# One fused attention-and-gate kernel: rows parted at 512 instead of 416, last part in chunks of 128, 128 and 32 rows, inverse roots spread through memory

## The chip, the cores and the metric

The kernel runs on one core of a Trainium2 chip. The metric is the device time in microseconds of the whole launch, the median of three runs. A span is the time from the first to the last instruction in one profiled execution; the launch takes a little more than its span.

## The reference

For 8 batches of N = 100 rows (R = 800 rows in all), width D = 1024, each with a memory of 722 rows of width 512:

```
memory_proj    = memory @ W_mem.T
attn           = softmax(hidden @ memory_proj.T / sqrt(D))
memory_context = attn @ memory_proj
gate           = sigmoid(concat(hidden, memory_context) @ W_gate.T + b_gate)
fused          = hidden + gate * memory_context
out            = fused * rsqrt(mean(fused**2, axis=-1) + 1e-6) * norm_w
```

All is float32. The last line needs, for each of the 800 rows, a mean over all 1024 columns before any value of that row can be written.

## The kernel before

Each float32 operand is split in a high part (rounded for TensorE's faster float32 form) and a low part, and each product is three matmuls: high by high, high by low, low by high (`three`, L314). The first 214 us of the span are the projections, the attention of the eight batches and the context times the memory weights. They are not changed.

Then comes the gate stage. Data lies transposed: partitions are columns of the model (KD = 8 tiles `t` of P = 128), the free dimension is the rows. The list `STEPS` sets its order: 17 steps `(t, r0, r1)`, each one tile of output columns for a range of rows, each 24 matmuls (8 tiles of the contraction, three products each) into one of two PSUM banks. The rows are in two parts, the first 416 rows and the last 384. The steps of the first part end at step END0 = 8; only (0, late) comes among them. Then follow the steps of the last part, the final one cut in 256 and 128 rows.

For each step, in pipeline with TensorE: ScalarE (ACT) takes the sigmoid out of PSUM (L694), seeds the bank of the step after next with the part of the gate that was made earlier (L700), takes squares (L713) and multiplies by norm_w in place (`weigh`, L704). VectorE (DVE) multiplies the gate by the context (L887), adds the input (`fuse`, L892) and adds the squares up (`sum_squares`, L875). `gate` and `square` have two buffers each, so a sigmoid waits for the fuse of two steps before, and a step's matmuls wait for their seed.

When all eight tiles of the first part are summed, TensorE makes its means (`mean_first`, L495, in the middle of step 10, after its contraction tile 4); DVE adds epsilon (L920), GpSimd (POOL) takes the power -1/2 (L969). These inverse roots lie by rows on partitions and are wanted along the free dimension on all partitions: DVE makes four diagonal matrices (L898), TensorE multiplies them by ones into bank RIB (`inverse`, L503, in the middle of step 11), and DVE multiplies each of the eight tiles by that bank (`output`, L904), two after each step from step 12 on. The sync engine (SP) stores two tiles at a time (L298), its queue in order: the last weight loads, then these four stores, then the row stores.

The last part ends by rows: TensorE makes the means of three chunks of 128 rows (L527, L532, L533) and transposes their tiles into PSUM (`turn`, L515); ACT scales the left half of the rows (L734) and DVE the right half (L949) by the inverse root into `row_out`, and SP stores each chunk of 512 KB (L302). The last wait of the kernel is for all stores.

Of the kernel before, what the change touches and what calls it, by code (L numbers as in the profile page):

```python
# [22 lines left out]
FIRST, CHUNK = 416, 128  # L23
ROWS2, LATE = (R - FIRST) // CHUNK, R - CHUNK
FC = FIRST // 4

TURN = ((0, 1), (2, 3), (5, 4))
# [9 lines left out]
    + [(t, FIRST, R) for t in range(1, KD - 1)] + [(KD - 1, FIRST, LATE), (KD - 1, LATE, R)]  # L37
# [8 lines left out]
def build(nc, xT, ctxT, ctxN, w_mem, w_gate_x, w_mem_t, w_gate_mc, b_gate, norm_w, outT, out_rows):  # L46
# [4 lines left out]
    with top:  # L51
# [47 lines left out]
        ones = sb(top, "ones", [P, P])  # L99
        minus_half = sb(top, "minus_half", [P, 4])  # L100
        rms = sb(top, "rms", [FC, 4])
        rms_late = sb(top, "rms_late", [CHUNK, ROWS2])
        rms_diag = sb(top, "rms_diag", [FC, 4, FC])
# [10 lines left out]
        row_out = x_again.rearrange("p k r -> p (k r)")[0:CHUNK, 0:ROWS2 * D]  # L114
# [69 lines left out]
        diag_done = sem("diag_done")  # L184
        inv_made = sem("inv_made")
        mean_w_set = sem("mean_w_set")
        late_mean_made = sem("late_mean_made")
        late_squared = sem("late_squared")
# [14 lines left out]
        def _(sp):  # L203
# [90 lines left out]
            for t in range(1, KD):  # L294
                load_w(J_G2 + t, w_gate_mc[t], t % 2)
            for k in range(0, KD, 2):
                sp.wait_ge(out_done, k + 2)
                sp.dma_start(out_v[:, k:k + 2, :], acc[:, k:k + 2, 0:FIRST]).then_inc(stored, 16)  # L298
            for i in range(ROWS2):
                sp.wait_ge(row_left, i + 1)  # L300
                sp.wait_ge(row_right, i + 1)
                sp.dma_start(out_rows[i * CHUNK:(i + 1) * CHUNK, :],  # L302
                             row_out[:, i * D:(i + 1) * D]).then_inc(stored, 16)
            sp.wait_ge(stored, 16 * (KD // 2 + ROWS2))
# [3 lines left out]
        def _(pe):  # L308
# [198 lines left out]
            def late_sums(i):  # L507
                at = FIRST + i * CHUNK
                return square_sum[:, at:at + CHUNK]

            def turn(i, t0, t1):

                at = FIRST + i * CHUNK
                for t in range(t0, t1):
                    done = nc.tensor.transpose(bank(TURN[i][t // 4], P, CHUNK, t % 4 * P), acc[:, t, at:at + CHUNK],  # L515
                                               ident[:, :])
# [487 lines left out]
```

## Time and profile before

| what | value |
|---|---|
| median of 3 runs | 298.63 us (298.62 to 299.34) |
| the profiled execution | 297.93 us |
| its span | 296.0 us, outside it 1.93 us |
| TensorE busy | 290.2 us, 98% |
| VectorE busy | 169.1 us, 57% |
| ScalarE busy | 159.9 us, 54% |
| gate stage, first matmul to last | 214.22 to 287.04 us |
| first and last row store issued | 290.38 and 292.16 us |

Times of instructions are microseconds from the start of the span. In the profile's rows PE is TensorE's matmul side, PEld its weight loads, SPq the sync engine's queue. Busy times of pipelined matmuls overlap, so the distance from one matmul's start to the next one's start, not the busy time, is what a matmul costs.

### The profile page before, as it was taken

What the parts mean: (1) busy time and instruction counts of PE and PEld (TensorE: products, weight loads), DVE (VectorE), ACT (ScalarE), POOL (GpSimd) and SP (SyncE); (2) the same over time, 40 slices, a digit from 0 to 9 for tenths busy, and PEclk for the clock granted to TensorE, in tenths of its full rate; (3) what the DMA queues carried; (4) which work ended last, traced back from release to release, by engine and by line L of the source; (5) the groups of instructions that cost most, each with busy time, mean ns of one, the idle gap of its engine ahead of it and who ended that gap; (6) DMA issues with size and microseconds to landing.
All of it is one profiled execution on the core that took longest, in us unless ns stands there. A gap on an engine that the chain in (4) does not pass through costs nothing.

```text
span 296.0 us, 4113 instructions
## 1 busy us (share of the span) xinstructions
PE 290.2 (98%) x1666; PEld 279.4 (94%) x1666; DVE 169.1 (57%) x234; ACT 159.9 (54%) x227; POOL 4.0 (1%) x10
## 2 busy tenths in 40 slices
PE   8999999999999999999999999999999999999993
PEld 8999999898999989899998989999999999999992
DVE  3658554558576575856657544422467662443663
ACT  5548435554574835448473526454367674543563
POOL 2000000000000000000000000000000000010001
PEclk9999999999999999999999999999999999999998
DMA  6999180884929569293966121086223400000235
GB/s 213 405 404 284 56 319 16 242 280 122 329 80 291 227 159 358 83 321 124 269 249 160 56 75 42 31 338 248 73 75 137 142 3 0 0 2 16 99 117 213
DMA packets 20930, 49.29 MB, mean 167 GB/s; under 512 B 2688, under 2 KB 4480, under 8 KB 20912
## 3 DMA queue, kind: packets, MB, share of 16 engines
q1 hardware_dynamic: 20912, 49.04, 49.4%
q8 instruction: 13, 0.21, 0.3%
q14 instruction: 5, 0.04, 0.0%
HBM read 45.49 MB, written 3.28 MB: 165 GB/s over the span
## 4 chain that ended last, share of the span: by engine, by line
PE 98%; DVE 0%; issue 0%; DVEq 0%
PE ps L314 70%; PE ps L408 11%; PE ps L431 9%; PE ps L422 1%; PE ps L435 1%; PE ps L328 1%; PE ps L442 1%; PE ps L515 1%; PE ps L503 0%; PE ps L339 0%; DVE x_again L949 0%; PE ps L345 0%; PE ps L349 0%; PE ps L342 0%; PE ps L354 0%; PE ps L351 0%
## 5 line engine op out<-in xcount | busy, mean ns | idle before, releaser
L314 PE MATMUL ps<-act_hi,w_hi 128*128 128x400 f32 (+4 forms) x272 | 79.8, 343 | 0.0
L314 PE MATMUL ps<-act_hi,w_lo 128*128 128x400 f32 (+4 forms) x272 | 79.0, 340 | 0.0
L314 PE MATMUL ps<-act_lo,w_hi 128*128 128x400 f32 (+4 forms) x272 | 78.9, 340 | 0.0
L314 PEld LDWEIGHTS ps<-act_hi,w_hi 128*128 128x128 f32 x272 | 49.9, 188 | 1.0
L314 PEld LDWEIGHTS ps<-act_lo,w_hi 128*128 128x128 f32 x272 | 50.6, 188 | 0.1
L314 PEld LDWEIGHTS ps<-act_hi,w_lo 128*128 128x128 f32 x272 | 50.6, 188 | 0.1
L741 DVE TENSOR_TENSOR w_lo<-w_stage,w_hi 128x1024 fp32r<-128x1024 f32 (+2 forms) x23 | 26.0, 1132 | 23.8 <-ACT w_hi L550 23.0
L741 DVE TENSOR_TENSOR cn_lo<-cn_stage,cn_hi 128x1536 fp32r<-128x1536 f32 (+1 forms) x16 | 23.8, 1486 | 7.2 <-ACT cn_hi L569 5.6
L741 DVE TENSOR_TENSOR ct_lo<-ct_stage,ct_hi 128x1444 fp32r<-128x1444 f32 x16 | 25.8, 1653 | 0.5 <-ACT ct_hi L561 0.5
L550 ACT ACTIVATE w_hi<-w_stage 128x1024 fp32r<-128x1024 f32 x20 | 21.0, 1054 | 6.0 <-PE ps L314 3.9
L637 ACT ACTIVATE pc<-ps,row_inv 100x512 f32<-100x512 f32 x8 | 5.5, 688 | 31.6 <-PE ps L435 31.6
L694 ACT ACTIVATE gate<-ps,bias_t 128x384 f32<-128x384 f32 (+3 forms) x15 | 8.6, 570 | 24.8 <-PE ps L314 24.7
L561 ACT ACTIVATE ct_hi<-ct_stage 128x1444 fp32r<-128x1444 f32 x16 | 21.7, 1405 | 0.0
L623 ACT ACTIVATE probs<-ps,neg_top 100x722 f32<-100x722 f32 x8 | 6.9, 865 | 27.2 <-DVE neg_top L820 27.2
L887 DVE TENSOR_TENSOR gate<-gate,mc 128x416 f32<-128x416 f32 (+3 forms) x17 | 9.3, 550 | 21.2 <-ACT gate L694 21.2
L408 PE MATMUL ps<-ct_hi,q_hi 128*100 128x362 f32 x64 | 21.4, 335 | 0.0
L408 PE MATMUL ps<-ct_hi,q_lo 128*100 128x362 f32 x64 | 21.0, 328 | 0.0
L408 PE MATMUL ps<-ct_lo,q_hi 128*100 128x362 f32 x64 | 21.0, 328 | 0.0
L741 DVE TENSOR_TENSOR act_lo<-mc,act_hi 128x800 fp32r<-128x800 f32 x8 | 7.9, 993 | 20.5 <-ACT mc L665 20.5
L314 PE MATMUL ps<-q_hi,w_hi 128*128 128x400 f32 x64 | 17.5, 344 | 0.0
L314 PE MATMUL ps<-q_lo,w_hi 128*128 128x400 f32 x64 | 17.5, 344 | 0.0
L314 PE MATMUL ps<-q_hi,w_lo 128*128 128x400 f32 x64 | 17.4, 344 | 0.0
(113 smaller groups left out, 459.9 us busy)
## 6 DMA issues: line engine op xcount, KB each, us to landing
ct_stage<-ctxT SPq DMA_DIRECT2D x16, 722.0 KB, 8.4
cn_stage<-ctxN SPq DMA_DIRECT2D x8, 768.0 KB, 5.8
cn_stage<-ctxN SPq DMA_DIRECT2D x8, 512.0 KB, 4.2
w_stage<-w_gate_x SPq DMA_DIRECT2D x8, 512.0 KB, 6.1
w_stage<-w_gate_mc SPq DMA_DIRECT2D x8, 512.0 KB, 3.5
x_again<-xT SPq DMA_DIRECT2D x1, 3200.0 KB, 11.5
cn_stage<-ctxN SPq DMA_DIRECT2D x8, 320.0 KB
acc<-xT SPq DMA_DIRECT2D x6, 400.0 KB, 7.4
```

The costliest lines, as they stand in the source:

```text
L314: done = nc.tensor.matmul(o, wgt, stream[h][part], start=first and wgt is wh and part == 0, stop=last and wgt is wl, skip_group_check=onto)
L328: nc.tensor.matmul(bank(7, P), idle_work[:, :], idle_work[:, :], start=True, stop=True)
L408: done = nc.tensor.matmul(bank(h, MH + 1, N), lhs[:, k, b * N:(b + 1) * N], rhs[:, k, at:at + MH + 1], start=k == 0 and part == 0, stop=k ...
L422: done = nc.tensor.transpose(o, probs[:, t * P:t * P + rows], ident[0:N, 0:N])
L431: nc.tensor.matmul(bank(PCB, C, N), lhs[:, t, :], rhs[:, t, :], start=t == 0 and part == 0, stop=False)
L550: nc.scalar.activation(w_hi[home][:, :], w_stage[:, slot, :], ACT.Copy).then_inc(w_hi_done, 1)
L561: nc.scalar.activation(ct_hi[:, 2 * s:2 * s + 2, :], ct_stage[:, 2 * s:2 * s + 2, :], ACT.Copy).then_inc(ct_hi_done, 1)
L623: nc.scalar.activation(probs[:, :].rearrange("p (h m) -> p h m", h=2), scores, ACT.Exp, bias=neg_top[:, :], scale=float(D) ** -0.5, accum_ ...
L637: nc.scalar.activation(pc[:, :], bank(PCB, C, N), ACT.Copy, scale=row_inv[:, :]).then_inc(pc_scaled, 1)
L694: nc.scalar.activation(part, part if n < 2 else gate_bank(n), ACT.Sigmoid, bias=bias_t[:, t:t + 1]).then_inc(gate_done, 1)
L741: return nc.vector.tensor_tensor(out, whole, hi.bitcast(F32), ALU.subtract)
L887: nc.vector.tensor_tensor(part, part, mc[:, t, r0:r1], ALU.mult).then_inc(gated, 1)
```

## The change

The first part has 512 rows and the last 288. The final step is no longer cut for TensorE, so there are 16 steps. The last part ends in chunks of 128, 128 and 32 rows (`CHUNKS`). Everything after the last matmul is done chunk by chunk: three sigmoids, three pairs of product and sum, squares on ACT instead of DVE, and means that add the sums of the tiles before to the squares of the last tile. The 32 rows of the small chunk are weighed into a buffer `small`, so that two transposes give 32 rows by 1024 columns on all 128 partitions as (row, quarter of the columns); their store is one contiguous piece of 128 KB. The means of the first part are made after contraction tile 1 of step 10, not tile 4. The inverse roots of the first part are stored to scratch memory `rms_rows` (128 by 4) and loaded back to all partitions (`rms_all`); the diagonals, the ones and the matmuls `inverse` are gone, and `output` reads `rms_all` with a step of four elements. The core of the diff:

```diff
...
-FIRST, CHUNK = 416, 128
-ROWS2, LATE = (R - FIRST) // CHUNK, R - CHUNK
...
+FIRST, SMALL = 512, 32
+CHUNKS = ((FIRST, FIRST + P), (FIRST + P, FIRST + 2 * P), (R - SMALL, R))
+PAIRS = P // SMALL
+NC = len(CHUNKS)
...
-TURN = ((0, 1), (2, 3), (5, 4))
+TURN, MEANS = ((0, 1), (2, 3), (5, 6)), (6, 7, 4)
...
-    + [(t, FIRST, R) for t in range(1, KD - 1)] + [(KD - 1, FIRST, LATE), (KD - 1, LATE, R)]
+    + [(t, FIRST, R) for t in range(1, KD)]
 LAST = len(STEPS) - 1
...
-        G2B, RIB = 4, 3
-
-        def late_mean(i, n=1):
-            return bank(6, n, CHUNK, 8 + i) if i < ROWS2 - 1 else bank(7, n, CHUNK, BANK - 1)
+        G2B = 4
+
+        def late_mean(i):
+            return bank(MEANS[i], 1, P, 8)
+
+        def small_part(t):
+            return small[:, t % 2, t // 2:P:PAIRS]
...
+            sp.wait_ge(rooted, 1)
+            sp.dma_start(rms_rows, rms[:, :]).then_inc(rms_stored, 16)
+            sp.wait_ge(rms_stored, 16)
+            sp.dma_start(rms_all[:, :], rms_rows.rearrange("p i -> (p i)").partition_broadcast(P)).then_inc(rms_in, 16)
             for k in range(0, KD, 2):
                 sp.wait_ge(out_done, k + 2)
                 sp.dma_start(out_v[:, k:k + 2, :], acc[:, k:k + 2, 0:FIRST]).then_inc(stored, 16)
...
+                if i < NC - 1:
+                    sp.dma_start(out_rows[i * P:(i + 1) * P, :],
+                                 row_out[:, i * D:(i + 1) * D]).then_inc(stored, 16)
+                else:
+                    sp.dma_start(out_rows[i * P:i * P + SMALL, :].rearrange("r (u c) -> (r u) c", u=PAIRS),
+                                 row_out[:, i * D:i * D + D // PAIRS]).then_inc(stored, 16)
...
-            def inverse():
-
-                pe.wait_ge(diag_done, 4)
-                for i in range(4):
-                    done = nc.tensor.matmul(bank(RIB, FC, P, i * FC), ones[0:FC, :], rms_diag[:, i, :],
-                                            start=True, stop=True)
-                done.then_inc(inv_made, 1)
...
+            def mean_of_sums(i):
+
+                a, b = CHUNKS[i]
+                pe.wait_ge(summed, LAST if i < NC - 1 else LAST + 1)
+                nc.tensor.matmul(late_mean(i), square_sum[:, a:b] if i < NC - 1 else small_sum[:, 0, :], mean_w[:, :],
+                                 start=True, stop=False)
+
+            def mean_of_last(i):
+
+                a, b = CHUNKS[i]
+                pe.wait_ge(squared, LAST + 1 + i)
+                nc.tensor.matmul(late_mean(i), square[:, LAST % 2, a - FIRST:b - FIRST] if i < NC - 1
+                                 else small_sum[:, 1, :], mean_w[:, :], start=False, stop=True)                    .then_inc(late_mean_made, 1)
...
+            def turn_small():
+
+                for j in range(2):
+                    done = nc.tensor.transpose(bank(TURN[NC - 1][j], P), small[:, j, :], ident[:, :])
                 return done
 
             for n in range(END0 + 2):
                 gate_mc(n)
-            gate_mc(END0 + 2, 4, mean_first)
-            gate_mc(END0 + 3, 4, inverse)
-            for n in range(END0 + 4, LAST + 1):
+            gate_mc(END0 + 2, 1, mean_first)
+            for n in range(END0 + 3, LAST + 1):
                 gate_mc(n)
-            pe.wait_ge(summed, LAST)
-            for i in range(ROWS2 - 1):
-                done = nc.tensor.matmul(late_mean(i), late_sums(i), mean_w[:, :], start=True, stop=True)
-            done.then_inc(late_mean_made, 1)
             pe.wait_ge(weighted, LAST)
-            turn(0, 0, KD).then_inc(turned, 1)
-            pe.wait_ge(late_squared, 1)
-            nc.tensor.matmul(late_mean(ROWS2 - 1), late_sums(ROWS2 - 1), mean_w[:, :], start=True, stop=False)
-            nc.tensor.matmul(late_mean(ROWS2 - 1), square[:, LAST % 2, 0:CHUNK], mean_w[:, :],
-                             start=False, stop=True).then_inc(late_mean_made, 1)
-            pe.wait_ge(out_done, KD)
-            turn(1, 0, KD).then_inc(turned, 1)
+            turn(0, 0, KD - 1)
+            mean_of_sums(0)
+            mean_of_sums(1)
+            turn(1, 0, 1)
+            mean_of_last(0)
+            turn(1, 1, 4)
+            mean_of_last(1)
             pe.wait_ge(weighted, LAST + 1)
-            turn(2, 0, KD).then_inc(turned, 1)
+            turn(0, KD - 1, KD).then_inc(turned, 1)
+            turn(1, 4, KD - 1)
+            mean_of_sums(2)
+            pe.wait_ge(weighted, LAST + 2)
+            turn(1, KD - 1, KD).then_inc(turned, 1)
+            mean_of_last(2)
+            pe.wait_ge(weighted, LAST + NC)
+            pe.wait_ge(mean_copied, 2)
+            turn_small().then_inc(turned, 1)
...
             def weigh(n):
                 t, r0, r1 = STEPS[n]
+                if r1 == R:
+                    nc.scalar.activation(small_part(t), acc[:, t, R - SMALL:R], ACT.Copy, scale=norm_t[:, t:t + 1])
+                    r1 = R - SMALL
                 nc.scalar.activation(acc[:, t, r0:r1], acc[:, t, r0:r1], ACT.Copy,
                                      scale=norm_t[:, t:t + 1]).then_inc(weighted, 1)
...
-            act.wait_ge(late_squared, 1)
-            weigh(LAST)
-            for i in range(ROWS2):
-                act.wait_ge(late_rooted, 1 + (i == ROWS2 - 1))
+            finish(LAST - 1)
+            act.wait_ge(gate_made, LAST + 1)
+            act.wait_ge(fused, LAST - 1)
+            for a, b in CHUNKS:
+                at = slice(a - FIRST, b - FIRST)
+                nc.scalar.activation(gate[:, LAST % 2, at], gate_bank(LAST)[:, at], ACT.Sigmoid,
+                                     bias=bias_t[:, KD - 1:KD]).then_inc(gate_done, 1)
+            act.wait_ge(summed, LAST - 1)
+            for i, (a, b) in enumerate(CHUNKS):
+                part = acc[:, KD - 1, a:b]
+                act.wait_ge(fused, LAST + 1 + i)
+                if i < NC - 1:
+                    nc.scalar.activation(square[:, LAST % 2, a - FIRST:b - FIRST], part,
+                                         ACT.Square).then_inc(squared, 1)
+                else:
+                    nc.scalar.activation(small_sum[:, 1, :].rearrange("p (r u) -> p r u", u=PAIRS),
+                                         part.unsqueeze(2).to_broadcast([P, SMALL, PAIRS]),
+                                         ACT.Square).then_inc(squared, 1)
+                act.wait_ge(squared, LAST + 1 + i)
+                nc.scalar.activation(part if i < NC - 1 else small_part(KD - 1), part, ACT.Copy,
+                                     scale=norm_t[:, KD - 1:KD]).then_inc(weighted, 1)
+            for i in range(NC):
+                act.wait_ge(late_rooted, i + 1)
                 act.wait_ge(turned, i + 1)
-                nc.scalar.activation(row_out[:, i * D:i * D + BANK], bank(TURN[i][0], BANK, CHUNK), ACT.Copy,
+                turned_left = bank(TURN[i][0], BANK if i < NC - 1 else P)
+                nc.scalar.activation(row_out[:, i * D:i * D + turned_left.shape[1]], turned_left, ACT.Copy,
                                      scale=rms_late[:, i:i + 1]).then_inc(row_left, 1)
...
-            def diagonals():
-                dve.wait_ge(rooted, 1)
-                for i in range(4):
-                    nc.vector.tensor_scalar(rms_diag[:, i, :], ident[0:FC, 0:FC], rms[:, i:i + 1], None,
-                                            ALU.mult).then_inc(diag_done, 1)
-
             def output(k):
 
-                rows = acc[:, k, 0:FIRST]
-                nc.vector.tensor_tensor(rows, rows, bank(RIB, FIRST), ALU.mult).then_inc(out_done, 1)
+                rows = acc[:, k, 0:FIRST].rearrange("p (i f) -> p i f", i=4)
+                nc.vector.tensor_tensor(rows, rows, rms_all.rearrange("p (f i) -> p i f", i=4),
+                                        ALU.mult).then_inc(out_done, 1)
...
             dve.wait_ge(mean_made, 1)
             nc.vector.tensor_scalar(rms[:, :], bank(6, 4, FC), EPS, None, ALU.add).then_inc(mean_copied, 1)
-            diagonals()
...
                 if n == END0 + 3:
                     dve.wait_ge(weighted, END0 + 1)
-                    dve.wait_ge(inv_made, 1)
+                    dve.wait_ge(rms_in, 16)
                 while done < min(KD, 2 * (n - END0 - 2)):
                     output(done)
...
+            for i, (a, b) in enumerate(CHUNKS):
+                part = gate[:, LAST % 2, a - FIRST:b - FIRST]
+                dve.wait_ge(gate_done, LAST + 1 + i)
+                nc.vector.tensor_tensor(part, part, mc[:, KD - 1, a:b], ALU.mult).then_inc(gated, 1)
+                dve.wait_ge(gated, LAST + 1 + i)
+                nc.vector.tensor_tensor(acc[:, KD - 1, a:b], part, x_again[:, KD - 1, a:b],
+                                        ALU.add).then_inc(fused, 1)
+            dve.wait_ge(summed, LAST)
+            nc.vector.tensor_copy(small_sum[:, 0, :].rearrange("p (r u) -> p r u", u=PAIRS),
+                                  square_sum[:, R - SMALL:R].unsqueeze(2).to_broadcast([P, SMALL, PAIRS]))                .then_inc(summed, 1)
+
+            def late_mean_plus_eps(i):
+                dve.wait_ge(late_mean_made, i + 1)
+                nc.vector.tensor_scalar(rms_late[:, i:i + 1], late_mean(i), EPS, None, ALU.add).then_inc(mean_copied, 1)
...
-            late_mean_plus_eps(1, ROWS2 - 1, 1)
-            for i in range(ROWS2):
-                right_half(i)
+            late_mean_plus_eps(0)
+            late_mean_plus_eps(1)
+            right_half(0)
+            late_mean_plus_eps(2)
+            right_half(1)
+            right_half(2)
...
```

## Rows read from the trace of the kernel before

**Rows 1.** The profile's first part (busy time, share, instructions), and the granted clock in 40 slices.

```profile
PE 290.2 (98%) x1666; PEld 279.4 (94%) x1666; DVE 169.1 (57%) x234; ACT 159.9 (54%) x227; POOL 4.0 (1%) x10
...
PEclk9999999999999999999999999999999999999998
```

**Rows 2.** Chain that ended last, in order of time: start, us, what.

```profile
261.75 0.65 PE ps L495 x8
...
266.73 0.87 PE ps L503 x8
...
289.42 1.82 PE ps L515 x16
...
291.33 0.75 DVE x_again L949
```

**Rows 3.** Timeline of ACT: start, us, instruction, idle time before and its releaser.

```profile
250.47 0.61 ACT L694 ACTIVATE gate<-ps,bias_t 128x416 f32<-128x416 f32 x1 [2.22 <-PE ps L314]
255.00 0.61 ACT L694 ACTIVATE gate<-ps,bias_t 128x416 f32<-128x416 f32 x1 [2.25 <-PE ps L314]
...
257.20 0.54 ACT L713 ACTIVATE square<-acc 128x416 f32<-128x416 f32 x1
...
273.52 0.58 ACT L694 ACTIVATE gate<-ps,bias_t 128x384 f32<-128x384 f32 x1 [2.01 <-PE ps L314]
...
277.73 0.58 ACT L694 ACTIVATE gate<-ps,bias_t 128x384 f32<-128x384 f32 x1 [2.01 <-PE ps L314]
```

**Rows 4.** Timeline of PE: first matmul of four steps, and the last of all.

```profile
254.74 0.34 PE L314 MATMUL ps<-act_hi,w_hi 128*128 128x384 f32 x1
...
281.69 0.28 PE L314 MATMUL ps<-act_hi,w_hi 128*128 128x256 f32 x1
...
284.53 0.22 PE L314 MATMUL ps<-act_hi,w_hi 128*128 128x128 f32 x1
...
287.04 0.28 PE L314 MATMUL ps<-act_hi,w_lo 128*128 128x128 f32 x1
```

**Rows 5.** Timeline of PE, 512 columns wide: the first and the 16th of one row of matmuls.

```profile
139.01 0.39 PE L431 MATMUL ps<-cn_hi,pt_hi 128*100 128x512 f32 x1
...
142.49 0.40 PE L435 MATMUL ps<-cn_hi,pt_hi 124*100 124x512 f32 x1
```

**Rows 6.** Timeline of DVE, second half of the gate stage.

```profile
257.76 0.59 DVE L875 TENSOR_TENSOR square_sum<-square_sum,square 128x416 f32<-128x416 f32 x1 [0.40 <-ACT square L713]
...
282.56 0.56 DVE L887 TENSOR_TENSOR gate<-gate,mc 128x384 f32<-128x384 f32 x1 [1.60 <-ACT gate L694]
...
284.10 1.08 DVE L904 TENSOR_TENSOR acc<-acc,ps 128x416 f32<-128x416 f32 x2
```

**Rows 7.** Groups of DVE by shape: count, busy us, mean ns, idle before.

```profile
L741 DVE TENSOR_TENSOR w_lo<-w_stage,w_hi 128x1024 fp32r<-128x1024 f32 x20 | 24.5, 1225 | 23.0 <-ACT w_hi L550 23.0
...
L904 DVE TENSOR_TENSOR acc<-acc,ps 128x416 f32<-128x416 f32 x8 | 4.3, 581 | 0.0
...
L741 DVE TENSOR_TENSOR w_lo<-w_stage,w_hi 128x512 fp32r<-128x512 f32 x1 | 0.7, 693 | 0.2 <-ACT w_hi L588 0.2
```

**Rows 8.** Timeline of POOL.

```profile
262.75 1.03 POOL L969 TENSOR_TENSOR rms<-rms,minus_half 104x4 f32<-104x4 f32 x1 [260.29 <-DVE rms L920]
...
289.69 0.55 POOL L973 TENSOR_TENSOR rms_late<-rms_late,minus_half 128x1 f32<-128x1 f32 x1 [0.69 <-DVE rms_late L936]
```

**Rows 9.** Timeline after the last step: the last tile's product, sum and weighing.

```profile
288.14 0.29 DVE L892 TENSOR_TENSOR acc<-gate,x_again 128x128 f32<-128x128 f32 x1
...
288.79 0.40 ACT L704 ACTIVATE acc<-acc,norm_t 128x128 f32<-128x128 f32 x1 [1.01 <-DVE square L944]
```

**Rows 10.** Timeline of SP's queue, the row stores.

```profile
290.38 2.11 SPq L302 DMA_DIRECT2D out_rows<-x_again  x3
```

**Rows 11.** DMA of 289 to 296 us in 40 slices, and the issues by line.

```profile
DMA  0000000000004999999999999999999999600000
GB/s 0 0 0 0 0 0 0 0 0 0 0 0 164 398 421 421 398 374 398 398 398 492 398 398 374 374 421 375 421 421 421 374 468 445 234 0 0 0 0 0
```

**Rows 12.** DMA issues of the whole span, in groups: KB each, us from issue to landing.

```profile
outT<-acc SPq DMA_DIRECT2D x4, 416.0 KB, 2.5
```

More of the change, by code:

```diff
@@ L98, in build @@
         mean_w = sb(top, "mean_w", [P, 1])
-        ones = sb(top, "ones", [P, P])
         minus_half = sb(top, "minus_half", [P, 4])
         rms = sb(top, "rms", [FC, 4])
-        rms_late = sb(top, "rms_late", [CHUNK, ROWS2])
-        rms_diag = sb(top, "rms_diag", [FC, 4, FC])
+        rms_late = sb(top, "rms_late", [P, NC])
+        small = sb(top, "small", [P, 2, P])
+        small_sum = sb(top, "small_sum", [P, 2, P])
+        rms_all = sb(top, "rms_all", [P, FIRST])
+        rms_rows = nc.dram_tensor("rms_rows", (FC, 4), F32, kind="Internal").ap()
         w_hi.append(sb(top, "w_hi2", [P, WB], F32R))
@@ L717, in _ @@
             act.wait_ge(gx_saved, 2 * B)
-            for n in range(LAST + 1):
+            for n in range(LAST):
                 if n in SPLIT_AT:
                     split_gate_w(SPLIT_AT[n])
-                early = n == END0 + 1 or n >= LAST - 1
+                early = n == END0 + 1
                 if early:
@@ L728, in _ @@
                     finish(n - 1)
-            act.wait_ge(late_squared, 1)
-            weigh(LAST)
-            for i in range(ROWS2):
-                act.wait_ge(late_rooted, 1 + (i == ROWS2 - 1))
+            finish(LAST - 1)
[19 more added lines that the diff above has]
+                                     scale=norm_t[:, KD - 1:KD]).then_inc(weighted, 1)
+            for i in range(NC):
+                act.wait_ge(late_rooted, i + 1)
                 act.wait_ge(turned, i + 1)
-                nc.scalar.activation(row_out[:, i * D:i * D + BANK], bank(TURN[i][0], BANK, CHUNK), ACT.Copy,
+                turned_left = bank(TURN[i][0], BANK if i < NC - 1 else P)
+                nc.scalar.activation(row_out[:, i * D:i * D + turned_left.shape[1]], turned_left, ACT.Copy,
                                      scale=rms_late[:, i:i + 1]).then_inc(row_left, 1)
@@ L847, in _ @@
             nc.vector.memset(mean_w[:, :], 1.0 / D).then_inc(mean_w_set, 1)
-            nc.vector.memset(ones[:, :], 1.0).then_inc(mean_w_set, 1)
             nc.vector.memset(minus_half[:, :], -0.5).then_inc(mean_w_set, 1)
@@ L933, in _ @@
             sum_squares(LAST - 1)
-            def late_mean_plus_eps(late, at, n):
-                dve.wait_ge(late_mean_made, late + 1)
-                nc.vector.tensor_scalar(rms_late[:, at:at + n], late_mean(at, n), EPS, None,
-                                        ALU.add).then_inc(mean_copied, 1)
-            gate_times(LAST)
-            late_mean_plus_eps(0, 0, ROWS2 - 1)
-            fuse(LAST)
-            part = acc[:, KD - 1, LATE:R]
-            dve.wait_ge(fused, LAST + 1)
-            nc.vector.tensor_tensor(square[:, LAST % 2, 0:CHUNK], part, part, ALU.mult).then_inc(late_squared, 1)
+            for i, (a, b) in enumerate(CHUNKS):
[5 more added lines that the diff above has]
+                                        ALU.add).then_inc(fused, 1)
@@ L964, in _ @@
             nc.gpsimd.memset(cn_stage[96:P, MT:MT + 2, :], 0.0).then_inc(spare_zeroed, 1)
-            pool.wait_ge(mean_w_set, 4)
+            pool.wait_ge(mean_w_set, 3)
             pool.wait_ge(mean_copied, 1)
             nc.gpsimd.tensor_tensor(rms[:, :], rms[:, :], minus_half[0:FC, :], ALU.pow).then_inc(rooted, 1)
-            for late, at, n in ((0, 0, ROWS2 - 1), (1, ROWS2 - 1, 1)):
-                pool.wait_ge(mean_copied, late + 2)
-                part = rms_late[:, at:at + n]
-                nc.gpsimd.tensor_tensor(part, part, minus_half[0:CHUNK, 0:n], ALU.pow).then_inc(late_rooted, 1)
+            for i in range(NC):
+                pool.wait_ge(mean_copied, i + 2)
+                part = rms_late[:, i:i + 1]
+                nc.gpsimd.tensor_tensor(part, part, minus_half[:, 0:1], ALU.pow).then_inc(late_rooted, 1)
 def kernel(x, ctx_1024, L0_xattn_W_mem, L0_xattn_W_gate, L0_xattn_b_gate, L0_xattn_norm_w):
```

28 lines of the change are left out of this document (11 added, 17 removed).

## The prediction

> **What bounds the kernel now.** I read the page first: TensorE is busy 98% of the span, at a granted clock of 9 tenths or more in all slices but the last [rows 1]. The reader should see that DVE (57%) and ACT have room on average, so that only two things can move the time: what TensorE is given to do, and what comes after its last matmul. The chain of waits says the same: it runs along TensorE to the transposes at 289.42, one DVE operation follows, and the rest is the store [rows 2]. The timeline of the gate stage shows no gap at the change of steps. So I price matmuls by the distance between starts.
>
> Per step of 24 matmuls: 416 columns take 4.53 us (255.00 less 250.47), 384 take 4.21 (277.73 less 273.52) [rows 3], 256 take 2.84 (284.53 less 281.69), and 128 take 2.62 (287.04 less 284.53 is 23 distances, 0.109 each) [rows 4]. Per matmul that is 189, 175, 118 and 109 ns. Halving 256 columns to 128 saves almost nothing: there the weight load sets the distance. All of the stage: 8 x 4.53 + 7 x 4.21 + 2.84 + 2.62 = 71.2 us, beside 1.5 us of other matmuls. I call T the end of the matmuls, 287.15 (287.04 + 0.11). From T to the end of the span are 8.85 us, and 1.93 us lie outside the span of this execution (297.93 us). The median is 0.7 above it; I carry my differences over to the median.
>
> **The new widths.** 512 columns: a row of matmuls in the attention has 15 distances in 3.48 us, 232 ns each [rows 5], so 5.57 us a step. Its weights have 100 columns and not 128, but at 232 ns a load is hidden either way. 288 columns: no row has them; between 256 (118) and 384 (175) the line gives 133 ns, 3.18 us a step. Bounds: 2.9 (the rate of 128 columns and the slope, were it bent) and 3.3. New sum: 8 x 5.57 + 8 x 3.18 = 70.0 us. **Gain 1.2 us**, of which nearly all is the step of 128 columns that is gone. With the bounds: from 0.2 to 2.
>
> **The matmuls of the inverse** are gone: 0.87 us in the chain [rows 2], all on TensorE. **Gain 0.87.** The memset of `ones` and the diagonals on DVE lay beside matmuls: nothing.
>
> **The means sooner.** They cost 0.65 [rows 2] for weights of 104 columns; with 128 about 0.75. Can they start? Before, the step after the first part starts at 254.74 [rows 4], its sigmoid 0.26 later, the last square at 257.20 [rows 3], the last sum at 257.76, ending 258.35 [rows 6], which is 3.6 after 254.74. The chain on ACT holds now a sigmoid, one square and one weighing of 512 columns and a seed of 288: +0.1 three times and -0.1; the last square and the last sum add 0.1 each. So the sum is ready at 4.0. TensorE comes there after one narrow step and six matmuls, 3.18 + 0.80 = 3.98, and loads weights 0.13 ahead. I take a stall of 0.15; bounds 0 and 0.6 (one more ACT operation ahead, such as the additional weighing of 32 columns that each late step now has). **Cost 0.25 with the wider weights.** Behind the wait stand all later matmuls, so it is paid in full.
>
> **The way through memory.** From the start of step 9: means made at 4.9, epsilon, then the power on POOL, 1.03 us [rows 8], 6.2; SP is past its weight loads and issues the store at 6.3. Behind the wait for it stand on SP only the output stores, which need the load anyway. No row has a store of 2 KB; the nearest is 416 KB in 2.5 us [rows 12]. I take 2.5 each for store and load (256 KB); bounds 1.5 and 5. `rms_all` is there at about 11.5. DVE wants it after the sum in step 11's pipeline: three narrow steps, the means, a sigmoid and three DVE operations, 12.7. So 1.2 us of cover, and DVE has more later (next paragraph). The wait costs nothing up to about 8.6 us for both, while gate products queue behind it on DVE.
>
> **DVE's load per narrow step.** Before, product to end of the two outputs is 282.56 to 285.18, 2.62 us in 4.21 [rows 6]. Now: three operations of 288 (about 0.46, distance 0.38 to 0.49) and two outputs of 512 columns. Contiguous, 512 columns take 0.69 [rows 7], distance 0.64: 2.5 us in a step of 3.18. Four such groups, steps 11 to 14; the last leaves DVE free at T+0.5 and the first chunk's sigmoid is done at T+0.64. Room in all: 3 x 0.68 + 0.15 = 2.2 us. But `rms_all` is read with a step of four elements, 16 bytes, and no row shows such a read. Bounds for one output: 0.69, and 1.22 for the row of 1024 columns [rows 7], as if each element cost two; beyond that a rival. I take 0.69, since all DVE rows here, from PSUM too (416 columns 0.58), go at one column in 1.04 ns [rows 7]. Cost 0.
>
> The Trainium skill (SBUF — State Buffer, section on the DMA port swizzle, its note on cachelines) says that lines are 16 bytes and that accesses which cross to a new line each time pay a penalty, full bandwidth needing two hits a line. No row here has it. By that rule every element of this read is a new line and the output goes up by an amount that the page doesn't give; it is rival A.
>
> **The tail.** Before, the first row store issues at T+3.2, the third at T+5.0 [rows 10], and data flows without a gap from 291.2 to 295.1 (T+7.95), 1.57 MB at about 400 GB/s [rows 11]: the stores' flow is the tail, once it has begun. After: sigmoid T+0.27 to 0.64; product and sum to 1.28 (0.29 each, distance 0.33 [rows 9]); ACT's square to 1.63; the mean's last matmul to 2.1; DVE is in the copy for the small chunk until 2.35, then epsilon to 2.5; POOL 0.55 [rows 8] to 3.15; the right half 0.75 [rows 2] to 3.9. First store T+4.0, later by 0.8. ACT's left half waits until its three squares and weighings (0.3 to 0.4 apart [rows 9]) are done at 3.25. Second chunk 4.85 (epsilon of the third goes ahead of it), third 5.25. TensorE's transposes (0.11 each [rows 2]) fit between. But only 1.18 MB are left to flow: 2.95 us from T+4.75 (0.8 after the issue) ends at T+7.7. **Gain 0.25**; bounds: -1.2 (each of the six waits between engines 0.25 later) and +0.6.
>
> **The sum.** -1.2 - 0.87 + 0.25 - 0.25 = -2.1 us: the profiled execution 295.9, the median 296.5 us.
>
> **Rivals.**
> A: the stepped read costs two columns' time each. 8 x 0.53 = 4.3 us more on DVE, less the room of 2.2: DVE comes to the last tile 2.1 late, the tail slides by it, 298.6 us, no change. For it: the read touches a line per element. Against: DVE's rate is the same from all its sources here, and that a second operand's fetch limits it is nowhere seen.
> B, the other side: the same read costs more still. With e us more per output, it is slower than before by 0.9 once 8e is over 2.2 + 2.1 + 0.9, so e over 0.65 and an output over 1.34 us. At 2.5 columns' time, e = 0.8: 6.4 - 2.2 = 4.2, 300.7 us. DVE would then be the bound of steps 11 to 14. Against: no DVE row goes slower than 1.4 ns per column.
> C: the tail's chain. ACT, DVE and TensorE hand over three chunks in a fixed order, and TensorE's in-order waits hold transposes back. At the bound, +1.45 against my sum, 298.0 us. For it: the chain before had four handovers for its last chunk, this one has them for each. Against: each is worked out above and stores overlap.
>
> **How the numbers follow.** Forecast 0.60, A 0.22, B 0.07, C 0.11. Less than 0.3% (0.9 us, 297.7 to 299.5) can't be told from no change. Faster: most of the forecast (0.58), 0.04 of C, 0.02 of A: 0.64. Same: 0.24. Slower: B, 0.04 of A, 0.01 of C: 0.12. Range 295.6 to 299.0; the forecast's own is 295.6 to 297.4.
>
> **What would show it.** A step of the first part 5.5 to 5.6 us between sigmoids, of the last 3.1 to 3.3; if 3.4, the widths gain nothing. L495's successor with a wait below 0.3 us before its weight load. Outputs of 128x512: 0.69 us right, 1.2 is A, over 1.34 is B. `rms_all` landing about 5 us after the power; if over 8.6, DVE stalls. First row store 4.0 us after the last gate matmul ends, data flowing to 7.7; if the last landing is later than before against T, C. The forecast is wrong if the median is above 297.7.

## The result and the profile after

The changed kernel takes 297.10 us (median of 6 runs, 296.70 to 297.55), the kernel before 298.62 (298.33 to 299.34). The ratio is 0.9947, 95% interval 0.9937 to 0.9958, so a gain of 1.3 to 1.9 us. Forecast were 296.5 and a gain of 2.1.

The page, and the sigmoids of two 512-column and two 288-column steps, to be compared with [rows 1, 3]:

```profile
PE 289.1 (98%) x1632; PEld 269.6 (91%) x1632; DVE 171.1 (58%) x231; ACT 161.0 (54%) x237; POOL 4.3 (1%) x11
...
PEclk9999999999999999999999999999999999999997
```

```profile
240.78 0.69 ACT L718 ACTIVATE gate<-ps,bias_t 128x512 f32<-128x512 f32 x1 [2.18 <-PE ps L328]
...
246.35 0.69 ACT L718 ACTIVATE gate<-ps,bias_t 128x512 f32<-128x512 f32 x1 [1.99 <-PE ps L328]
...
273.71 0.50 ACT L718 ACTIVATE gate<-ps,bias_t 128x288 f32<-128x288 f32 x1 [1.13 <-PE ps L328]
...
276.91 0.50 ACT L718 ACTIVATE gate<-ps,bias_t 128x288 f32<-128x288 f32 x1 [1.13 <-PE ps L328]
```

A step of 512 columns takes 5.57 us between sigmoids, one of 288 takes 3.20. Then the ends of the stage, on PE (start, us):

```profile
266.68 0.29 PE L328 MATMUL ps<-act_hi,w_lo 128*128 128x288 f32 x1
266.86 1.05 PE L509 MATMUL ps<-mean_w,square_sum 128*128 128x1 f32 x8
267.77 0.38 PE L328 MATMUL ps<-act_hi,w_hi 128*128 128x288 f32 x1
...
286.09 0.30 PE L328 MATMUL ps<-act_hi,w_lo 128*128 128x288 f32 x1
```

The gate matmuls end at T = 286.09 + 0.13 = 286.22. They began at 215.01, where before they began at 214.22; nothing ahead of that point is changed, and other profiles of the same kernel begin the stage at 214.60 and 214.42. So the stage is read by its length: 71.21 us against 72.93, **1.72 us less**. The store of the roots, their load and DVE's steps (SP, then DVE):

```profile
269.49 0.33 SPq L303 DMA_DIRECT2D rms_rows<-rms  x1
271.43 0.33 SPq L305 DMA_DIRECT2D rms_all<-rms_rows  x1
...
290.79 1.06 SPq L313 DMA_DIRECT2D out_rows<-x_again  x2
```

```profile
275.11 0.45 DVE L921 TENSOR_TENSOR square_sum<-square_sum,square 128x288 f32<-128x288 f32 x1
275.48 2.10 DVE L944 TENSOR_TENSOR acc<-acc,rms_all 128x512 f32<-128x512 f32 x2
277.46 0.49 DVE L933 TENSOR_TENSOR gate<-gate,mc 128x288 f32<-128x288 f32 x1
...
285.16 2.12 DVE L944 TENSOR_TENSOR acc<-acc,rms_all 128x512 f32<-128x512 f32 x2
287.19 0.46 DVE L921 TENSOR_TENSOR square_sum<-square_sum,square 128x288 f32<-128x288 f32 x1
287.56 0.29 DVE L977 TENSOR_TENSOR gate<-gate,mc 128x128 f32<-128x128 f32 x1
```

The reader should see that two outputs of 512 columns take 2.1 us, not 1.3, that DVE goes from the outputs at once into the next product from 277.46 on, without the idle time that ended at 282.56 in [rows 6], and that the product of the last tile's first chunk starts at 287.56, 1.34 us after T. The chain that ended last ran along TensorE up to one last DVE operation before [rows 2]; now it leaves TensorE four steps of the last part before T, and from 275.11 on it is DVE's up to the inverse roots of the last rows (start, us, what):

```profile
267.91 5.71 PE ps L328 x42
...
286.17 1.11 DVE acc L944
287.28 0.37 DVE square_sum L921
...
291.39 0.37 ACT x_again L781
```

The first row store is issued at T+4.57 (290.79) and the span ends at T+9.4, before T+3.2 and T+8.85. **The tail (all that comes after T) costs 0.5 us more**, where 0.25 less was forecast.

### The profile page after: what moved, and what is told of

It reads as the page before. It is cut to its first block, busy times and chain, and to the rows that moved or that the text cites. A ratio compares the mean times of both kernels' runs of the same rounds, so it can differ in the third digit from the quotient of the medians.

```text
span 295.6 us, 4053 instructions
## 1 busy us (share of the span) xinstructions
PE 289.1 (98%) x1632; PEld 269.6 (91%) x1632; DVE 171.1 (58%) x231; ACT 161.0 (54%) x237; POOL 4.3 (1%) x11
## 4 chain that ended last, share of the span: by engine, by line
PE 92%; DVE 4%; issue 1%; POOL 0%; ACT 0%; POOLq 0%; DVEq 0%; ACTq 0%
PE ps L328 65%; PE ps L422 11%; PE ps L445 9%; DVE acc L944 2%; PE ps L436 1%; PE ps L342 1%; PE ps L449 1%; PE ps L456 1%; DVE square_sum L921 1%; DVE gate L933 1%; PE ps L353 0%; POOL rms_late L1021 0%; PE ps L509 0%; PE ps L356 0%; DVE acc L979 0%
## 5 line engine op out<-in xcount | busy, mean ns | idle before, releaser
L328 PE MATMUL ps<-act_hi,w_hi 128*128 128x400 f32 (+2 forms) x264 | 78.0, 347 | 0.0
L328 PE MATMUL ps<-act_hi,w_lo 128*128 128x400 f32 (+2 forms) x264 | 77.2, 344 | 0.0
L328 PE MATMUL ps<-act_lo,w_hi 128*128 128x400 f32 (+2 forms) x264 | 77.2, 344 | 0.0
L328 PEld LDWEIGHTS ps<-act_hi,w_hi 128*128 128x128 f32 x264 | 48.4, 188 | 2.7
L328 PEld LDWEIGHTS ps<-act_hi,w_lo 128*128 128x128 f32 x264 | 49.0, 188 | 1.8
L328 PEld LDWEIGHTS ps<-act_lo,w_hi 128*128 128x128 f32 x264 | 49.0, 188 | 1.8
L933 DVE TENSOR_TENSOR gate<-gate,mc 128x512 f32<-128x512 f32 (+1 forms) x15 | 8.7, 583 | 19.5 <-ACT gate L718 19.5
L718 ACT ACTIVATE gate<-ps,bias_t 128x288 f32<-128x288 f32 (+1 forms) x13 | 7.6, 585 | 21.7 <-PE ps L328 21.7
```

Source lines behind the costliest of these rows:

```text
L328: done = nc.tensor.matmul(o, wgt, stream[h][part], start=first and wgt is wh and part == 0, stop=last and wgt is wl, skip_group_check=onto)
L718: nc.scalar.activation(part, part if n < 2 else gate_bank(n), ACT.Sigmoid, bias=bias_t[:, t:t + 1]).then_inc(gate_done, 1)
L933: nc.vector.tensor_tensor(part, part, mc[:, t, r0:r1], ALU.mult).then_inc(gated, 1)
```

## The experiments

Times below are medians; "of before" is the ratio to the runs of the kernel before on the same chip, with its 95% interval. T is always the start of the last gate matmul plus one distance. A line "..." in a diff marks what is left out of it.

**The changed kernel again.** No edit.

> The changed kernel as it is, run again beside the others. Both theories: 297.1 us. In its first profile the gate stage began 0.8 us later than before (215.02 against 214.22) although nothing ahead of it is changed; if that is chance, the stage begins near 214.2 here and the span is about 294.8; if it is part of the change, near 215.0 again.

297.37 us, 0.9957 of before (0.9942 to 0.9971). Its stage starts at 214.60 and is 71.21 us long; the first product stands at T+1.33, the first store at T+4.56, the end at T+9.4. The later start in the first profile doesn't repeat; the length of the stage, the first product and the first store repeat to 0.02 us.

**Contiguous reads, by the order of TensorE's weights.**

```diff
-                    ... square_sum[:, i * FC:(i + 1) * FC], mean_w[:, :],
+                    ... square_sum[:, i:FIRST:4], mean_w[:, :],
...
-                rows = acc[:, k, 0:FIRST].rearrange("p (i f) -> p i f", i=4)
-                ... rms_all.rearrange("p (f i) -> p i f", i=4), ALU.mult)
+                rows = acc[:, k, 0:FIRST]
+                ... rms_all[:, :], ALU.mult)
```

> The changed kernel with one thing else: the means take every fourth row as weights, so that the scratch memory holds the roots in the order of the rows and DVE's eight outputs read rms_all contiguously. Theory (DVE's stepped reads of 1.08 us leave it 0.7 us late at the last tile, and the tail slides by that): outputs 0.69 us, the last tile's first product 0.65 us after the last gate matmul instead of 1.34, 0.7 us faster than the changed kernel, 296.4. Rival (the stores' flow is the tail, so a late start of it is made up): outputs 0.69 but 297.1. Rival (weights read in steps cost TensorE what DVE gains): the eight matmuls of the first means over 1.3 us instead of 0.9, 297.0.

298.05 us, 0.9992 of before (0.9971 to 1.0014): no gain on the kernel before, where the changed kernel beside it had 0.9957. DVE did what the theory said:

```profile
287.90 1.29 DVE L944 TENSOR_TENSOR acc<-acc,rms_all 128x512 f32<-128x512 f32 x2
...
289.65 0.29 DVE L976 TENSOR_TENSOR gate<-gate,mc 128x128 f32<-128x128 f32 x1
```

T is 289.05, so the first product is at T+0.60, the first store (292.89) at T+3.84, the end at T+8.7: a tail 0.7 shorter. But TensorE lost more. Timeline of PE around the means, and PE in stretches (us, busy, granted clock, DMA):

```profile
267.19 2.03 PE L509 MATMUL ps<-mean_w,square_sum 128*128 128x1 f32 x8
269.08 0.38 PE L328 MATMUL ps<-act_hi,w_hi 128*128 128x288 f32 x1
...
269.49 0.44 PE L328 MATMUL ps<-act_hi,w_lo 128*128 128x288 f32 x1
269.73 0.44 PE L328 MATMUL ps<-act_hi,w_hi 128*128 128x288 f32 x1
```

```profile
263.18:266.35 3.17, 3.17 (x25) 1.00 0.00 0
269.29:272.50 3.21, 3.21 (x15) 0.51 0.02 1
```

The eight passes of weights read with a step of four take 1.9 us instead of 0.9, and right after them TensorE runs for 3.2 us at a granted clock of 0.51, its lower level of 1.2 GHz: 15 matmuls of 288 columns where the earlier stretch of the same length has 25, their starts 0.24 us apart and not 0.133. The stage is 73.71 us long, 2.50 more than the changed kernel's: 1.0 of it lies in the passes, the other 1.5 in the matmuls at the lower clock. The twelve runs fall in two groups, five of 299.4 to 299.7 and seven of 297.0 to 298.05. The profile is of the first; that the clock fell at the same place in the other four isn't shown (only their mean clocks are on record, 0.987 in three and 0.992 in one). The seven have a median of 297.7, which is the changed kernel's 297.4 with 1.0 more on TensorE and 0.7 less in the tail. So the third view of the expectation held, and something on top of it that none had.

**The old way of spreading the roots, in the new kernel.** Diagonals on DVE, ones by diagonals on TensorE in step 11 after contraction tile 4, outputs read from PSUM:

```diff
-            for n in range(END0 + 3, LAST + 1):
+            gate_mc(END0 + 3, 4, inverse)
+            for n in range(END0 + 4, LAST + 1):
...
-                ... rms_all.rearrange("p (f i) -> p i f", i=4), ALU.mult)
+                ... bank(RIB, FIRST), ALU.mult)
...
```

> The changed kernel with the old way of spreading the inverse roots: diagonals on DVE, ones by diagonals on TensorE in the middle of step 11, outputs from PSUM. Theory: TensorE has about 1.0 us more (four matmuls of 128 by 128 instead of 104), the outputs of 512 from PSUM take 0.68 us, so the tail is 0.7 earlier: 297.4, slower than the changed kernel by 0.3 us or no different. Rival (the way through memory is worth its whole 0.9 and the stepped read costs nothing): 298.0.

297.85 us, 0.9972 of before (0.9959 to 0.9985), 0.5 slower than the changed kernel beside it. Its stage is 0.9 longer (215.49 to 287.60), its outputs 0.60 apart, its first product at T+0.60 (288.20) and its first store at T+3.84 (291.44). The median alone doesn't choose between the two views, 297.4 and 298.0; the profile does: the product is in time, as the theory said. But TensorE's 0.9 and the tail's 0.7 don't cancel as far as it said. The end stands at T+8.95 and not at T+8.7 as with the contiguous reads above: of the 0.7 at the first store only 0.4 reach the end, so 0.5 are lost. The last store is issued at the same T+4.99 in both and lands 0.3 later here; why, is open.

**The way through memory alone, in the kernel before.**

```diff
-            gate_mc(END0 + 3, 4, inverse)
-            for n in range(END0 + 4, LAST + 1):
+            for n in range(END0 + 3, LAST + 1):
...
+            sp.dma_start(rms_rows, rms[:, :]) ...
+            sp.dma_start(rms_all[:, :], rms_rows.rearrange("p i -> (p i)").partition_broadcast(P)) ...
...
+                ... rms_all.rearrange("p (f i) -> p i f", i=4), ALU.mult)
```

> The kernel before with one part of the change alone: 416 rows, old tail, but the inverse roots through scratch memory with the stepped read. Theory: the inverse's 0.87 us leave TensorE and the outputs of 416, about 0.91 us each (1.80 ns a column), stay hidden, since two of them and the rest are 3.3 us in a step of 4.21: 297.7, 0.9 faster than before. Rival (a slower output slides the tail whenever it stands ahead of the last tile): 298.3 or more.

298.17 us, 0.9984 of before (0.9967 to 1.0001), so a gain of 0 to 1 us that isn't clear of none. In the profile the stage is 72.03 us, 0.90 less than before, and a pair of outputs takes 1.72 to 1.75 us:

```profile
284.12 1.75 DVE L890 TENSOR_TENSOR acc<-acc,rms_all 128x416 f32<-128x416 f32 x2
285.78 0.43 DVE L879 TENSOR_TENSOR gate<-gate,mc 128x256 f32<-128x256 f32 x1
```

T is 287.18. The product of the 256 columns, at 285.39 or T-1.76 before, stands at T-1.40, and the first row store at T+3.49 against T+3.2. I had called the outputs hidden; they are in the steps of 4.21 us but not ahead of the short step that ends the stage, so about 0.3 of the 0.9 goes back in the tail.

**Order made by the store.** `rms_rows` is held as 4 by 128, so the store has 512 pieces of 4 bytes, and the load and DVE are contiguous:

```diff
...
-            sp.dma_start(rms_rows, rms[:, :]) ...
+            sp.dma_start(rms_rows.rearrange("i f -> f i"), rms[:, :], ...) ...
...
```

> The changed kernel with contiguous outputs again, but the order is made by the store: rms goes to scratch memory as 512 pieces of 4 bytes and rms_all is read contiguously; TensorE's weights stay as in the changed kernel. Theory (the stepped read makes DVE 0.7 us late and the tail slides by it): outputs 0.65 us apart, the last tile's first product 0.60 us after the end of the gate matmuls, first row store at 3.84 after it, and 0.7 us faster than the changed kernel: 296.5, provided the store lands within about 3 us (1.4 to 1.9 with pieces of 16 bytes). Rival (the tail is bound by the stores' flow, not by DVE): no faster than the changed kernel, 297.2. Rival (the scattered store takes over 5 us): DVE waits at the first output, 297 or more.

303.98 us, 1.0172 of before (1.0159 to 1.0185). The third view held, and by far more than I had thought. Views of SP, and of the scratch memory's landings (store and load together: least, median, most), then DVE:

```profile
269.45 0.38 SPq L303 DMA_DIRECT2D rms_rows<-rms  x1
278.70 0.33 SPq L305 DMA_DIRECT2D rms_all<-rms_rows  x1
```

```profile
DMA to landing us min/median/max: 4.6/6.9/9.2
```

```profile
283.38 1.30 DVE L944 TENSOR_TENSOR acc<-acc,rms_all 128x512 f32<-128x512 f32 x2 [7.87 <-DMA rms_all<-rms_rows]
...
292.26 0.29 DVE L976 TENSOR_TENSOR gate<-gate,mc 128x128 f32<-128x128 f32 x1
```

The store took 9.2 us to land instead of 1.4 to 1.9, and DVE, with the gate's products queued behind, waited 7.9 us. It answers nothing on the stepped read, but it is the prediction's paragraph on the way through memory from its far side. Its limit for store and load was 8.6 us, they take 13.8 here, so the first product should slide by 5.2; it starts at 292.26, T+6.09, 5.5 later than with DVE in time (T+0.60). What follows adds to it: the end is at T+15.9, 6.6 after the changed kernel's.

**The means at tile 4 again.**

```diff
-            gate_mc(END0 + 2, 1, mean_first)
+            gate_mc(END0 + 2, 4, mean_first)
```

> The changed kernel with one part undone: the first means after contraction tile 4 of step 10 as before, not tile 1. Theory: TensorE's short wait before the means (about 0.15 us) goes, but means, roots and rms_all come 1.2 less 0.15 us later, at about 275.6 to 276 where DVE wants it at 275.1 to 275.5; DVE has no room with the stepped read, so up to 0.5 us go into the tail: 0.1 to 0.4 us slower than the changed kernel, 297.5. Rival (the means sooner cost more in TensorE's wait than they bring): faster by 0.15, 297.0.

298.13 us, 0.9985 of before (0.9969 to 1.0002). The runs fall in two groups, seven of 296.9 to 298.1 and five of 299.0 to 299.6 with a lower mean granted clock (0.987 or 0.988 against 0.991 to 0.994); the changed kernel had one such run (298.3, 0.989) in each of its two series of 10 and 12. In the profile, from the first group, the wait is as forecast (timeline of DVE):

```profile
275.75 2.12 DVE L944 TENSOR_TENSOR acc<-acc,rms_all 128x512 f32<-128x512 f32 x2 [0.44 <-DMA rms_all<-rms_rows]
```

DVE waits 0.44 us for `rms_all`; T is 285.96 and the first product starts at 287.84, T+1.88 against T+1.34. TensorE's passes for the means start without a gap:

```profile
267.76 0.29 PE L328 MATMUL ps<-act_hi,w_lo 128*128 128x288 f32 x1
267.90 0.95 PE L509 MATMUL ps<-mean_w,square_sum 128*128 128x1 f32 x8
268.70 0.38 PE L328 MATMUL ps<-act_hi,w_hi 128*128 128x288 f32 x1
```

From gate matmul to gate matmul they take 0.94 us here and 1.09 in the changed kernel, with the same weights of 128 columns, so the wait that the earlier place costs is 0.15; the stage is 0.14 shorter. The theory holds in the profile; the median moved more than its 0.1 to 0.4 because of the second group. No profile is of that group, and why it comes so often here is open.

**512 rows alone, in the kernel before.**

```diff
-FIRST, CHUNK = 416, 128
+FIRST, CHUNK = 512, 96
```

> The kernel before with 512 rows in the first part and the rest of the last part as it was: three chunks of 96 rows, the final step cut in 192 and 96 columns. Theory (the gain of the widths is the cut step that is gone, nothing of it the 512): 8 x 5.57 + 7 x 3.19 + 2 x 2.64 = 72.2 us of gate matmuls against 71.2 before, so about 1 us slower than before, 299.6, less up to 0.2 for smaller stores. Rival (wide steps save in themselves): no slower than before, 298.6 or less.

300.18 us, 1.0044 of before (1.0031 to 1.0057), 1.4 us slower. The stage is 74.06 us (214.95 to 289.01), 1.13 longer than before: the theory's 1.0. Two short steps that end the stage cost more than they hold in columns: with 192 columns and with 96 the matmuls start 0.11 us apart, as with 128.

**Strides by themselves.** A stride is the step between the elements that an operation reads or writes. One run, with operations behind the kernel's own work, on DVE 256 columns of float32, on ACT 128:

> The changed kernel with operations behind its work, for their durations alone (the time of the whole says nothing): products of 256 float32 columns on DVE with the second operand stepped by 1, 2, 3, 4, 5, 8 and 16 elements, with both stepped by 4, with the output stepped by 4; tensor_scalar with 1, 4 and 16; copies of 128 on ACT with 1, 2, 4 and 16 and with a stepped output; fp32 weights on TensorE with 1, 2, 4 and 6. Theory (a step of 16 bytes or more costs a second access per element): 0.43 us up to a step of 3, 0.62 (1.80 ns a column) from 4 on and no more for 16; both operands stepped the same or double. Rival (the cost grows with the step): step 2 already dearer than 1 and 16 dearer than 4. TensorE's weights: 0.11 us each with step 1, 0.24 with 4.

Timeline of DVE, in the order second operand stepped by 1, 2, 3, 4, 5, 8 (not shown, 0.62), 16; both by 4; output by 4; then `tensor_scalar` with 1, 4, 16:

```profile
291.10 0.41 DVE L1019 TENSOR_TENSOR x_again<-mc 128x256 f32<-128x256 f32 x1
291.43 0.42 DVE L1020 TENSOR_TENSOR x_again<-mc 128x256 f32<-128x256 f32 x1
291.77 0.50 DVE L1021 TENSOR_TENSOR x_again<-mc 128x256 f32<-128x256 f32 x1
292.19 0.61 DVE L1022 TENSOR_TENSOR x_again<-mc 128x256 f32<-128x256 f32 x1
292.72 0.61 DVE L1023 TENSOR_TENSOR x_again<-mc 128x256 f32<-128x256 f32 x1
...
293.78 0.59 DVE L1025 TENSOR_TENSOR x_again<-mc 128x256 f32<-128x256 f32 x1
294.28 0.62 DVE L1026 TENSOR_TENSOR x_again<-mc 128x256 f32<-128x256 f32 x1
294.81 0.63 DVE L1027 TENSOR_TENSOR x_again<-mc 128x256 f32<-128x256 f32 x1
295.25 0.30 DVE L1028 TENSOR_SCALAR x_again<-mc 128x256 f32<-128x256 f32 x1
295.46 0.40 DVE L1029 TENSOR_SCALAR x_again<-mc 128x256 f32<-128x256 f32 x1
...
```

The cost is a plateau from four elements (16 bytes) on: 0.61 us against 0.41, no dearer for 16 elements, both operands or the output. Two elements cost nothing (0.42), three cost 0.50, where 0.43 was expected. `tensor_scalar` goes from 0.30 to 0.40 and 0.38 (the row left out). On ACT (step 1, 4 and 16; step 2 takes 0.30, the output by 4 0.41):

```profile
291.22 0.31 ACT L792 ACTIVATE gate<-mc 128x128 f32<-128x128 f32 x1
...
291.64 0.42 ACT L794 ACTIVATE gate<-mc 128x128 f32<-128x128 f32 x1
291.96 0.41 ACT L795 ACTIVATE gate<-mc 128x128 f32<-128x128 f32 x1
```

TensorE's weights said nothing: less than hoped: the engine ran there at its lower clock (granted 0.50), where every load took 0.33 us. Passes start 0.213 us apart with steps of 1 and 2, 0.233 with 4 and 0.222 with 6, so at that clock a step of 4 costs 0.02 a pass. At full clock the kernel with stepped weights above has the same 0.234, where the contiguous passes of the changed kernel stand 0.112 apart.

**The last two outputs cut to 8 columns,** beside the changed kernel once more. The kernel leaves out the other 504 columns of these two products, so those values of the result stay without their inverse root.

```diff
+                cols = FC if k < KD - 2 else 2
-                rows = acc[:, k, 0:FIRST].rearrange("p (i f) -> p i f", i=4)
+                rows = acc[:, k, 0:FIRST].rearrange("p (i f) -> p i f", i=4)[:, :, 0:cols]
```

> The changed kernel as it is, as the reference for the two beside it: 297.2 us.

> The changed kernel, but of the last two of the eight outputs only 8 of 512 columns are computed, so that rows 0 to 511 of the last 256 columns of the result are wrong but for a few. All else, the stores too, is the same. It takes 1.8 us off DVE just ahead of the last tile and nothing off the other engines. Theory (DVE comes 0.7 us late to the last tile because of its stepped reads, and the tail slides by it): first product 0.60 us after the end of the gate matmuls, first row store 3.84 after it, the whole 0.7 faster than the changed kernel beside it. Rival (the stores' flow or the hand-overs between engines set the tail): no more than 0.2 faster.

296.39 us, 0.9931 of before (0.9914 to 0.9948), against 297.50 and 0.9959 (0.9947 to 0.9972) of the changed kernel: 0.8 us by the ratios. DVE:

```profile
285.04 0.46 DVE L921 TENSOR_TENSOR square_sum<-square_sum,square 128x288 f32<-128x288 f32 x1
286.47 0.29 DVE L978 TENSOR_TENSOR gate<-gate,mc 128x128 f32<-128x128 f32 x1 [0.98 <-ACT gate L761]
```

It idles 0.98 us for ACT's sigmoid. T is 285.87: product T+0.60, first store (289.72) T+3.85, end T+8.6, all 0.7 earlier than in the changed kernel. The edit changes DVE's load, and with it only when the last column store is issued (285.1, at T-0.8 instead of T+1.1). That store doesn't set the tail: with contiguous reads, with the diagonals and in the experiment that follows it goes out at T+0.2, and the first row store stands at T+3.84 or T+3.85 all the same. So the slide of the tail is DVE's lateness.

**Contiguous reads, by the order of one sum.** DVE's last sum of squares of the first part writes in the order of the roots into a free stage buffer, the means stand after tile 3, and the outputs read `rms_all` contiguously:

```diff
+                if n == END0:
+                    rows, squares = (a.rearrange("p (f i) -> p i f", i=4) for a in (rows, squares))
+                    sums = sums_by_root.rearrange("p (i f) -> p i f", i=4)
...
-                    ... square_sum[:, i * FC:(i + 1) * FC], mean_w[:, :],
+                    ... sums_by_root[:, i * FC:(i + 1) * FC], mean_w[:, :],
-            gate_mc(END0 + 2, 1, mean_first)
+            gate_mc(END0 + 2, 3, mean_first)
...
```

> The changed kernel with contiguous outputs by a third way: DVE's last sum of squares of the first part reads with a step of four and writes the sums in the order of the roots, so TensorE's weights, the store in pieces of 16 bytes and the outputs' reads are all contiguous; the means stand after contraction tile 3, not 1, to give that sum its time. One stepped operation (about 1.08 us) in place of eight. Theory: no wait before the means, rms_all at most 0.3 us later than before and covered, outputs 0.69 us, tail 0.7 earlier: 0.7 to 0.9 faster than the changed kernel, 296.4. Rival (later means bring rms_all too late for DVE): the first output waits over 1 us, and the gain shrinks below 0.3.

296.36 us (295.99 to 296.99), 0.9932 of before (0.9915 to 0.9949), and 0.8 us faster than the changed kernel beside it by the ratios: the fastest of all complete kernels here. Timeline of DVE:

```profile
265.55 1.11 DVE L928 TENSOR_TENSOR w_stage<-square_sum,square 128x512 f32<-128x512 f32 x1 [0.26 <-ACT square L741]
...
274.95 1.29 DVE L951 TENSOR_TENSOR acc<-acc,rms_all 128x512 f32<-128x512 f32 x2
...
286.12 0.29 DVE L983 TENSOR_TENSOR gate<-gate,mc 128x128 f32<-128x128 f32 x1
```

One stepped operation of 1.11 us stands in place of eight, DVE waits less than 0.2 us for `rms_all`, and with T at 285.51 the product is at T+0.61, the first store at T+3.85, the end at T+8.6.

## Why the prediction was right, and where it was off

- *The new widths, gain 1.2.* Right: 5.57 and 3.20 us a step against 5.57 and 3.18. That it is the cut step's end and not the 512 rows is shown by 512 and 96 alone, which lose 1.13 us of the stage. The bound on the good side was added up wrongly: eight steps of 2.9 us would have given a gain of 3.4, not 2.
- *The matmuls of the inverse, gain 0.87.* Right: 0.90 in the kernel before, 0.9 in the changed one.
- *The means sooner, cost 0.25.* Right: from the last matmul ahead (266.68) to the next gate matmul (267.77) are 1.09 us, less one distance 0.96, against 0.65 before, so 0.3. With the means at tile 4, where nothing waits, it is 0.81. So half of the 0.3 is the wait, 0.15 as forecast, and half the wider weights, 0.15 where 0.1 was forecast. The stage as a whole: forecast -1.8, measured -1.72.
- *The way through memory, no cost.* Right: 1.9 and 3.5 us to landing against 2.5 and 2.5, the load there at 275.0, DVE ready at 275.5. The cover was 0.5 and not 1.2: counted from the start of step 9 (262.85) DVE was ready after 12.6, near the 12.7 forecast, but the store was issued at 6.6 instead of 6.3, and the two landings took 5.5 instead of 5.0. With the means at tile 4 the wait of 0.44 appears.
- *DVE's load, cost 0.* **This step failed, by the size of one term.** I took 0.69 us for a stepped output, with 1.22 as the other end, and rival A at 1.22. Measured: 1.07 to 1.11, mean 1.09. That is 0.39 more for each of eight, 3.1 us against a room that I had at 2.2; 0.9 should be left, 0.74 was (T+1.34 against T+0.60). The reason that I gave for 0.69, that all DVE rows run at one column in 1.04 ns, was no evidence, because no row had such a step. The rule of the Trainium skill (SBUF — State Buffer, section on the DMA port swizzle, note on cachelines) pointed the right way: the trace and the strides by themselves agree that a step of one 16-byte line costs, and larger ones no more. Its condition, two hits a line, fits what was measured: a step of 2 elements is free, one of 4 pays in full. Its "how far you can stride for free", 4 elements of float32, isn't borne out: 3 cost already. That note gives no amount; here it is 0.20 us on 0.41 for 256 columns.
- *The tail, gain 0.25.* As a mechanism right: with DVE in time (two outputs cut, or the permuted sum) the first store is at T+3.85 against 4.0 and the end at T+8.6, where 7.7 + 0.9 was the forecast. In the changed kernel it starts 0.7 later and the gain becomes a loss of 0.5.
- *Rivals.* A happened at three quarters of its price: the time lies between the forecast and A. B and C did not: no stepped output came near 1.34 us, and with DVE in time the three row stores are issued at T+3.85, 4.58 and 5.01, where 4.0, 4.85 and 5.25 were worked out. (B's "no DVE row goes slower than 1.4 ns per column" misread its own rows: 128 columns in 0.29 us [rows 9] are 2.3 ns each, the fixed part of a short operation counted in.) The sum without A's part: -1.72 - 0.2 = -1.9; with it -1.2 by the stage and the tail of the profile. The medians gave -1.5 at first, and by the ratios -1.3 and -1.2 in the two repeats, whose 297.4 and 297.5 stand at the upper end of the forecast's own range. The 0.3 more at first is within what the start of the stage alone wanders (214.2 to 215.5 in the thirteen profiles).

## What to carry to other kernels

A layout change is paid where it is read most: eight stepped operations on an engine with 0.7 us of room per step gave back a third of the gain, and one stepped operation ahead of them (the permuted sum) took it back. When work is shortened on the bounding engine, price the others against the new, shorter step, not against the old share of busy time. And a last step that is cut for the tail's sake doesn't get cheaper with its columns: 128 columns cost 2.62 us where 256 cost 2.84, and 96 no less than 128.

## What was not expected of the hardware

- TensorE's granted clock dropped in the middle of the gate stage. In the one profile that shows it, of the kernel with stepped weights, TensorE did nothing but eight passes of one column for 1.9 us, then ran at 0.51 for 3.2 us. Of the other runs only the mean clock is known. It was 0.989 or less in four of 12 runs of that kernel, in 2 of 28 runs of the changed kernel, in one of 12 of the way through memory alone, and in five of 12 with the means at tile 4, where the passes take only 0.8 us. So the length of the passes doesn't sort the runs, and the cause is open.
- A store of 2 KB in 512 pieces of 4 bytes landed in 9.2 us (one profile), in 128 pieces of 16 bytes in 1.4 to 1.9.
- Weights of TensorE read with a step of 16 bytes took about 0.24 us a pass at full clock instead of 0.12.
- `tensor_scalar` of 256 columns out of SBUF takes 0.30 us where a product of two tensors takes 0.41.
